# Attention's denominators by transposed block sums on VectorE instead of matmuls with a block of ones

## The reference

```python
q = elu(q * E ** -0.5) + 1 + 1e-4        # E = 32 features of a head
k = elu(k) + 1 + 1e-4
def step(carry, qkv_t):                  # over the tokens, one after the other
    kv_s = kv_s + einsum('bhe,bhf->bhef', k_t, v_t)
    k_s  = k_s + k_t
    num  = einsum('bhe,bhef->bhf', q_t, kv_s)
    den  = einsum('bhe,bhe->bh', q_t, k_s)[..., None] + 1e-6
    return (kv_s, k_s), num / den
```

## Time and profile before

| | |
|---|---|
| time, median of 3 runs (lowest, highest) | 2054.0 us (2053.19, 2054.0) |
| span of the profiled execution | 2051.8 us; its own time is not listed apart, the median lies 2.2 us above the span |
| PE busy | 2021.4 us (99%) |
| DVE busy | 1545.5 us (75%) |
| ACT busy, POOL busy | 1002.8 us (49%), 955.4 us (47%) |
| granted TensorE clock, mean | 0.998 of full speed |

### The profile page before, as it was taken

One profiled execution on the slowest core, in us unless ns is written; L12 is line 12 of the kernel. 1 busy time (PEld: TensorE's weight loads), 2 busy tenths in 40 slices (PEclk: granted clock), 3 DMA queues, 4 the chain that ended last, 5 costly groups with the idle time before them and its releaser, 6 DMA issues. The chain is left out here.

```text
span 2051.8 us, 44446 instructions
## 1 busy us (share of the span) xinstructions
PE 2021.4 (99%) x16388; PEld 1646.2 (80%) x16388; DVE 1545.5 (75%) x2228; ACT 1002.8 (49%) x1733; POOL 955.4 (47%) x782
## 2 busy tenths in 40 slices
PE   7999999999999999999999999999999999999999
PEld 4688888888888888888878888888888888888887
DVE  7988888888988988888885755857567475774744
ACT  5444554555554455545453545535464353643533
POOL 2635544555545455444534343443434444344444
PEclk9999999999999999999999999999999999999999
DMA  7011222322222322222266465655556556465443
GB/s 261 32 58 45 81 84 89 99 94 61 91 88 83 99 73 83 78 88 83 73 230 222 149 206 180 205 183 170 192 170 206 182 177 195 148 215 183 164 166 107
DMA packets 157163, 276.80 MB, mean 135 GB/s; under 512 B 11105, under 2 KB 35681, under 8 KB 157026
## 3 DMA queue, kind: packets, MB, share of 16 engines
q1 hardware_dynamic: 156498, 273.73, 40.1%
q10 hardware_dynamic: 528, 1.05, 0.1%
HBM read 208.67 MB, written 66.06 MB: 134 GB/s over the span
## 5 line engine op out<-in xcount | busy, mean ns | idle before, releaser
L1641 POOL TENSOR_TENSOR h_lo<-y_rows,h_hi 128x512 fp32r<-128x512 f32 x192 | 246.5, 1302 | 366.2 <-ACT h_hi L1739 366.1
L904 DVE RECIPROCAL r_den<-r_den 128x512 f32<-128x512 f32 x64 | 213.7, 3341 | 0.4 <-ACT r_den L613 0.4
L437 POOL TENSOR_TENSOR x_res<-y,x_res 128x512 f32<-128x512 f32 x64 | 83.1, 1299 | 221.7 <-DVE y L930 211.0
L909 DVE TENSOR_TENSOR probs<-sc,causal 128x512 f32<-128x512 f32 x256 | 158.5, 680 | 7.6 <-PE sc L1275 7.6
L600 ACT ACTIVATE z_exp<-pj,qk_neg 128x512 f32<-128x512 f32 x128 | 87.8, 686 | 149.3 <-PE pj L1247 142.2
L426 POOL TENSOR_TENSOR a_lo<-a_t,a_hi 128x512 fp32r<-128x512 f32 x60 | 81.0, 1350 | 170.8 <-ACT a_hi L628 170.8
L2069 PE MATMUL sc<-wd,h_hi 128*128 128x512 f32 x384 | 150.7, 392 | 0.0
L1247 PE MATMUL pj<-xt_hi,w_hi 128*128 128x512 f32 x512 | 146.5, 408 | 4.0 <-DVE xt_lo L876 2.0
L2069 PE MATMUL sc<-wd,h_lo 128*128 128x512 f32 x384 | 149.6, 390 | 0.0
L1247 PE MATMUL pj<-xt_lo,w_hi 128*128 128x512 f32 x512 | 139.4, 394 | 1.8 <-DVE xt_lo L876 1.8
L1854 DVE TENSOR_TENSOR r_den<-pj,k_tok 128x512 f32<-128x512 f32 x96 | 66.3, 691 | 98.3 <-ACT k_tok L1722 54.0
(11 more groups left out here) (261 smaller groups left out, 5678.9 us busy)
## 6 DMA issues: line engine op xcount, KB each, us to landing
w_hi<-parts SPq DMA_DIRECT2D x48, 1024.0 KB, 5.3
w_lo<-parts SPq DMA_DIRECT2D x48, 1024.0 KB, 5.2
x_mid<-x_res SPq DMA_DIRECT2D x96, 256.0 KB, 2.7
x_res<-in_L_attn_x SPq DMA_DIRECT2D x64, 256.0 KB, 2.7
xg<-in_L_attn_x SPq DMA_DIRECT2D x15, 1024.0 KB, 7.1
x_res<-x_mid SPq DMA_DIRECT2D x60, 256.0 KB, 4.0
full<-x_mid SPq DMA_DIRECT2D x60, 256.0 KB, 3.7
parts<-r_den SPq DMA_DIRECT2D x48, 256.0 KB, 2.3
```

What stands on the lines that cost most here:

```text
L437: pool.tensor_tensor(out=x_res[:, slot, :], in0=y[:, :], in1=x_res[:, slot, :], op=ALU.add).then_inc(y_ready, 1)
L904: dve.reciprocal(r_den[parity][:, c, :], r_den[parity][:, c, :]).then_inc(rden_ready, 1)
L909: dve.tensor_tensor(out=probs[:, h, :].rearrange("p (c i) -> p c i", c=C), in0=sc[:, h, :].rearrange("p (c i) -> p c i", c=C), in1=causal[ ...
L1641: pool.tensor_tensor(out=h_lo[b], in0=h[i], in1=h_hi[b].bitcast(F32), op=ALU.subtract).then_inc(h_lo_ready, 1)
```

## The change

POOL's product `prod` stays, with two buffers. `prod_high`, `prod_low`, `denominators`, `den_out` and the matrix of ones go. DVE now sums over the 32 features of a head in one instruction for each block `c`: `den_of` reads 128 x 512 as blocks of 32 x 32, transposes each and sums along the row, which leaves 128 x 16 values: tokens on partitions. `recip` adds the epsilon (three small instructions, which also swap the two halves of the partitions for the odd blocks) and takes the reciprocal of 128 x 64 values, once in a group. `spread`, once in a tile, transposes 32x32 blocks again, of a source read with stride zero, which copies a head's reciprocal to its 32 partitions for 128 x 512 values (`r_heads`); `divide` reads that. The odd blocks' heads are now turned by two places instead of one. Code of other groups that could never run was dropped from the programs' text; it issued nothing.

```diff
     def num_part(tile, t, c, h):
-        to = (h + c % 2) % HPC
+        to = (h + HPC // 2 * (c % 2)) % HPC
...
         def q_times_sum(g, parity, c):
             wait(pool, ksum_ready, g * C + c + 1)
             wait(pool, phi_ready, g * 2 * C + 2 * c + 2)
-            wait(pool, prod_lo_ready, g * C + c)
-            pool.tensor_tensor(out=prod[:, :], in0=k_sum[:, c % 2, :], in1=qt[parity][:, c, :],
+            wait(pool, den_ready, g * C + c - 1)
+            pool.tensor_tensor(out=prod[:, c % 2, :], in0=k_sum[:, c % 2, :], in1=qt[parity][:, c, :],
                                op=ALU.mult).then_inc(prod_ready, 1)
-        def prod_low(g, c):
...
-        def prod_high(g, c):
...
-        def den_out(g, parity, c, bank):
...
-        def recip(g, parity, c):
-            wait(dve, den_ready, g * C + c + 1)
-            dve.reciprocal(r_den[parity][:, c, :], r_den[parity][:, c, :]).then_inc(rden_ready, 1)
+        def den_of(g, c):
+            wait(dve, prod_ready, g * C + c + 1)
+            dve.tensor_reduce(den[:, c, :], prod[:, c % 2, :].rearrange("p (b i) -> p b i", i=E), AX.X, ALU.add,
+                              apply_transpose=True).then_inc(den_ready, 1)
+        def recip(g, parity):
+            wait(dve, den_ready, (g + 1) * C)
+            even, odd = (slice(0, C, 2), slice(1, C, 2))
+            low_half, high_half = slice(0, P // 2), slice(P // 2, P)
+            dve.tensor_scalar(den_eps[:, even, :], den[:, even, :], EPS_DEN, None, ALU.add).then_inc(den_chain, 1)
+            for to, of in ((low_half, high_half), (high_half, low_half)):
+                dve.tensor_scalar(den_eps[to, odd, :], den[of, odd, :], EPS_DEN, None, ALU.add).then_inc(den_chain, 1)
+            wait(dve, den_chain, g * 3 + 3)
+            dve.reciprocal(r_tok[:, parity, :, :], den_eps[:, :, :]).then_inc(rden_ready, 1)
+        def spread(tile, g, parity, t):
+            wait(dve, rden_ready, g + 1)
+            wait(dve, a_ready, tile)
+            blocks_of_t = r_tok[:, parity, :, t * (P // E):(t + 1) * (P // E)].rearrange("p c (b a) -> p c b a", a=1)
+            dve.transpose(r_heads.rearrange("p (c b i) -> p c b i", c=C, i=E),
+                          blocks_of_t.broadcast_to([P, C, P // E, E])).then_inc(r_spread, 1)
...
         def divide(tile, g, parity, t):
             wait(dve, num_ready, tile + 1)
-            wait(dve, rden_ready, (g + 1) * C)
+            wait(dve, r_spread, tile + 1)
...
-        def denominators(g, c, bank):
-            wait(pe, prod_lo_ready, g * C + c + 1)
-            wait(pe, den_ready, g * C + c)
-            pe.matmul(bank, head_ones[:, c % 2, :], prod_hi[:, :], start=True, stop=False)
-            pe.matmul(bank, head_ones[:, c % 2, :], prod_lo[:, :], start=False, stop=True).then_inc(den_ps, 1)
```

More of the change, by code:

```diff
@@ L748, in group @@
         def group(g, parity):
[L749 to L754, removed]
+            if not (isinstance(g, int) and g == NG - 1):
                 return ahead_of_last(g, parity)
-            if ahead:
-                exp_relu(n, 0)
-                exp_relu(n, 1)
             k_rows(g * GT)
[L761 to L764, removed]
+            for op in (B11, B21):
+                for k in range(2):
+                    high(0, op, k)
@@ L1012, in vector @@
         v_rows(0, 0, 0)
-        recip(0, 0, 0)
+        den_of(0, 2)
         feature(0, 0, 7)
@@ L1063, in ahead_of_last @@
             mask(g * GT + 2)
+            spread(g * GT + 2, g, parity, 2)
             feature(n, other, 5)
-            recip(n, other, 0)
+            den_of(n, 1)
             feature(n, other, 6)
@@ L1076, in ahead_of_last @@
             v_rows(n, other, 0)
-            recip(n, other, 1)
+            spread(g * GT + 3, g, parity, 3)
+            den_of(n, 3)
             v_rows(n, other, 1)
@@ L1103, in group @@
             v_rows(g, parity, 3)
-            recip(g, parity, 3)
-            if ahead:
-                feature(n, other, 0)
-            if isinstance(g, int) and g == 0:
-                recip(0, 0, 2)
-            if not last:
-                recip(g, parity, 3)
-            if last:
-                norm_stats(NG + 1, range(2))
+            spread(g * GT, g, parity, 0)
+            norm_stats(NG + 1, range(2))
             gate_last(g, 0)
             divide(g * GT, g, parity, 0)
-            if last:
-                norm_stats(NG + 1, range(2, 3))
-                a_low(g * GT)
-                norm_stats(NG + 1, range(3, GT))
-                norm_var(NG + 1)
@@ L1144, in group @@
-            if ahead:
-                feature(n, other, 4)
+            norm_x(NG + 1, range(1))
+            a_low(g * GT + 1)
+            norm_x(NG + 1, range(1, GT))
             mask(g * GT + 2)
-            if ahead:
-                feature(n, other, 5)
-                recip(n, other, 0)
-                feature(n, other, 6)
+            spread(g * GT + 2, g, parity, 2)
             gate_last(g, 2)
-            if last:
-                sum_of(0, T1, 0)
+            sum_of(0, T1, 0)
             divide(g * GT + 2, g, parity, 2)
-            if last:
-                sum_of(0, T2, 0)
-                a_low(g * GT + 2)
@@ L1185, in group @@
-            if ahead:
-                v_rows(n, other, 2)
-            if two_ahead:
-                xt_low(g + 2, parity, 3)
-            if ahead:
-                recip(n, other, 3 if near_last else 2)
-            if last:
-                sum_of(0, T2, 1)
-                a_low(g * GT + 3)
+            sum_of(0, T2, 1)
+            a_low(g * GT + 3)
         groups(dve, 2, NG - 2, group)
@@ L1396, in rest @@
             ahead = not isinstance(g, int) or g + 1 < NG
-            if t == 3 and ahead:
-                wait(pe, probs_ready, tile * HPC + 3)
-                denominators(g + 1, 2, den_bank)
             if not ahead and t + 1 < GT:
@@ L1403, in rest @@
                 out_project(tile - 1)
-            if t in (1, 2) and ahead:
-                wait(pe, probs_ready, tile * HPC + 3)
-                denominators(g + 1, t - 1, den_bank)
             if t >= 2 and ahead:
                 x_turn(g + 2, 2 * t - 3, x_bank)
-            if t == 3 and ahead:
-                denominators(g + 1, 3, den_bank)
             if ahead:
```

227 lines of the change are left out of this document (45 added, 182 removed).

## The result

The changed kernel takes 2021.4 us (median of four runs, 2021.2 to 2022.4) against 2054.0 before: a ratio of 0.984, 95% interval 0.983 to 0.986. The profiled execution spans 2019.9 us, 31.9 less than before; forecast were 27.5 less.

A forecast was written before the change was run, and what follows sets the result against it. PE's matmul list was taken to bound attention, with DVE's tile 1 touching it at unit 6. Loop 16.9, groups 0, 1 and 14 5.6, start 5: 27.5 us off the 2051.8 span, so about 2027 us median; range 2015 to 2043.

The forecast's parts named there:

- PE's part: Denominators of four blocks leave PE's list, 0.47 us each, 1.88 us in each of 15 groups; new head turn costs nothing.
- The price of the new DVE instructions: `den_of` and `spread` 0.70 us each, 64-column reciprocal 0.42 us and about a tenth more, additions near 0.17 us.
- Rivals 3 and 4: Tile 1's DVE list: 3, it becomes the bound, slower, 2060 to 2088, chance 0.08; 4, no effect, chance 0.04.
- Rival 4: No effect: the new DVE pair at 1.7 to 2.0 us each gives all back, 2050 to 2058 us; chance 0.04.
- Tile 1: DVE ahead of `gate_last`: 1.4 us added, about 1.2 of 1.75 us stretching regained, merge up to 0.5; 0.7 under free 0.89.
- rival 2: Tile 1 grows on DVE: stretching stays, 0.55 us a group, 2033; instructions at 1.2 us, 2039; both 2045; chance 0.20.
- The fixed 6.7 us from `gate_last` to the division: In tile 1, from `gate_last` at 539.64 to the division's end at 546.37 nothing changes; it hangs on `out_project`'s end.
- The loop, 1.41 us a group: 1.88 us saved less 0.47 us longer wait at unit 6; 12 groups give 16.9 us.
- The start, 5 us: Late first division, half-speed matmuls, `xt_lo` wait and denominators go, 7.6 us at most; `norm_x` costs against it; 5 taken.
- The last group loses only work that waits anyway: The last group was to bring no gain from the change.
- Rival 1: PE's whole list is saved, nothing touches in tile 1: 36 to 38 us less, 2016 to 2018 us; chance 0.11.

The follow-up runs named there:

- the pairs put back: Changed kernel with two matmuls of 128x128 by 128x512 put back at each of the four places where the denominators stood, result unread: 2043.5 us, ratio 0.995.
- the run with short reciprocals: Kernel before, with each DVE reciprocal cut from 512 to 64 columns, PE's, ACT's and POOL's work as before: 2045.8 us, ratio 0.996.
- the ten further kernels: Follow-up kernels with the changed kernel's start; tile 1 of group 0 comes between 80.33 and 82.85 us in them, 81.87 in the changed kernel.
- four moves that removed the wait at unit 6, or nearly: Changed kernel with `norm_x` behind the division, 2056.2 us; second `word_size` behind tile 2's mask, 2033.3; POOL's residual behind `a_low`, 2023.2; `norm_x` ahead of `gate_last`, 2012.1.
- `norm_x`'s run: Changed kernel with `norm_x` of tile 1 moved behind the division of tile 1: 2056.2 us, ratio 1.002.
- one kernel of the thirteen: Changed kernel with tile 1's block sum done three times in the loop, the two extra ones behind `gate_last`: 2033.0 us, ratio 0.990.

## Why the prediction was right, point by point

- **PE's part.** 0.47 us for a block: `k_turn` starts 0.92 us after the last row of `out_project`, and the 0.47 are gone. With the pairs put back a loop group lost 1.35 us of its gain of 1.54, and the run with short reciprocals shows that DVE's relief alone gives 0.12. The new turn of the heads cost nothing: from `k_turn` to the scores of the next tile it is 2.45 us in tile 1 (519.80 to 522.25) and was 2.47.
- **The price of the new DVE instructions.** 0.70 us taken, 0.706 and 0.685 measured. The reciprocal of 64 columns is 0.55 instead of 0.46, the additions 0.17 and 0.18. Rivals 3 and 4 fell with this: the pair costs 1.4 us, far from 3.9. (Rival 4's own terms give 2048 to 2056, and not 2050 to 2058.)
- **Tile 1.** Unit 6 is the one place of the loop where PE waits, and it eats the saving of tile 1 as forecast: 0.54 us late instead of 0.07. Right was that POOL's subtraction stretched the scan, and that `gate_last` keeps air. But I had 0.2 to 0.7 us less air, and it is 0.06 more: both stretched rows shrank by 1.79 us together, not 1.2, because the bias was over in time; against that stand 1.23 us for the new pair, by starts, and 0.52 for the first merge. How much hangs on this step is shown in part: with POOL's subtraction back, 1.14 us of stretching met 0.95 us of idle time and cost 0.08 us a group. What the rest of it, which rival 2 priced at 0.55, would have cost was not tried.
- **The fixed 6.7 us from `gate_last` to the division.** Right in length, wrong in what it is. I took it for DVE's own work; about 0.6 of it are waiting for POOL's residual, hidden in the time of a merge (0.81 us with that wait, 0.16 without). A block sum fits in there for nothing.
- **The loop, 1.41 us a group.** 1.54 measured. The missing 0.13 is mostly the wait of the scores of tile 3 for `gate_last`, a row of the waits that I passed over; it went with the reciprocals, and the run with short reciprocals shows it alone (16.37 to 16.27). In 12 groups 1.6 us.
- **The start, 5 us.** This term was sized too small: 4.33 + 5.67 - 1.88 = 8.1 us, where 5 was taken and 7.6 was the upper end. I had taken off for `norm_x` of group 1, which was to miss turns with POOL. It did begin 1.3 us later, at 56.42 instead of 55.16; but it was over by 61.6 instead of 60.9, and PE waited 0.44 us ahead of the transpositions where I feared 3 us and a spell of lower clock. This is 3.1 of the 4.4 us between forecast and result. With the starts of the ten further kernels in place of this one, the term is 7.1 to 9.7 us against the one trace of the kernel before. So 5 was too small; that the term passed its upper end of 7.6 is not certain.
- **The last group loses only work that waits anyway:** not quite. Its tile 0 is shorter, 9.77 us instead of 10.78, but its tile 1 is longer, 7.88 instead of 7.18, and from tile 2 on it is 0.5 us longer. PE waits there for `a_lo`, behind the division (in tile 2 it was 0.98 us and is 1.41), and `spread` now stands ahead of both. That `spread` is the cause was not tried.

Rival 1, the whole list saved, was 2016 to 2018. The version with `norm_x` ahead of `gate_last` is that rival made true, and reaches 2012, because start and loop were worth more as well: 8.9 us instead of at most 7.6, and 27.5 instead of 25.0.

## What to carry to other kernels

Work taken off the bounding engine is saved only up to the next place where that engine meets another: follow its list to each wait, and see how late the other side's instruction ends there. That instruction's time may itself be a wait, as the merge of 128 values was for POOL. Before moving an instruction to make room, look at what its new neighbours release on the engine that it takes turns with, and who waits for it: of four moves that removed the wait at unit 6, or nearly, two put another in its place that cost more than the one removed, one broke even, and the one that filled idle time alone won 9 us.

## What the runs showed of the hardware that I had not expected

- A transposition of 32x32 blocks of a source read with stride zero costs 0.706 us for 128x512, and a sum over the partitions of each block in the same instruction as its transposition 0.685: as much as a plain read of that size (0.670).
- The merge of 128 values took between 0.16 and 0.81 us, by when POOL's instruction ended.
- The wait of 2.1 us in `norm_x`'s run set the granted clock to the lower of its levels in seven groups of the loop; waits just as long in the other five did not.
- At the loop's turn, one kernel of the thirteen had DVE stand for 3.4 us without a releaser, five times, each time with two packets of a queue for instructions starting 0.3 to 0.7 us later; in the other kernels that queue is still from 330 to 905 us, and DVE does not stand.
